# Shared expert in groups of 512 tokens with stationary first-layer weights, and the first routed expert's weights split during attention

## The chip, the cores and the metric

One NeuronCore of a Trainium2 chip runs the program. The metric is the device time of one execution in microseconds (us), and the median of three runs stands for the kernel. Before the change it is 575.73 us (575.15 to 580.42).

## The reference

A batch of 8 x 256 tokens (2048) of width D = 256 passes a gated cross-attention and then a gated mixture of experts:

```python
x = x + tanh(g_xattn) * attention(layernorm(x), ctx)      # 16 heads of 16, 77 keys per batch
n = layernorm(x).reshape(2048, 256)
w, sel = top_k(softmax(n @ gate_w.T), 2); w = w / w.sum(-1)
h = gelu(einsum('th,ehf->tef', n, W1) + b1); y = einsum('tef,efh->teh', h, W2) + b2
out = einsum('teh,te->th', y, combine(w, sel))            # 8 experts, F = 1024
out = out + gelu(n @ sW1 + sb1) @ sW2 + sb2               # shared expert, every token
x = x + tanh(g_ffn) * out
```

All is float32. The kernel computes only the two chosen experts of each token.

## The kernel before

**Attention.** It runs over 16 tiles of 128 tokens (NT = 16), software pipelined: `step(t)` on each engine does the scores of tile t + 1, the softmax of tile t, the projection of tile t - 1 and the second norm and the routing logits of tiles t - 2 to t - 4. GpSimd writes the normalised row block `x2row` (`normal_two`, L461); it first waits until the store of the block before it has landed. SP stores it to `x2`, and in the last seven steps SP also writes zeros into the DRAM tensor `routed_x`. GpSimd also loads the shared expert's weights in quarters and makes their low parts. Every weight and activation of the experts is held as a high part, rounded to fp32r, and a low part (the rest), and a product is hi x lo + hi x hi + lo x hi.

**The experts.** The work is one list of 55 tiles of 128 rows: NA = 9 early tiles of the shared expert, NR = 39 routed tiles (tokens sorted by expert in `routed_x`, padded to tiles), NB = 7 late tiles of the shared expert. All have the same form. `turn_rows` transposes the rows (L722), ACT rounds them and DVE takes the rest. `up` (L741 to L743) has the rows stationary and streams the weights: for each half of F, 2 x 3 matmuls of 512 columns. DVE adds the bias (L1277), ACT applies gelu (L1117). As the result has tokens on the partitions, `turn_hidden` transposes it in 8 pieces (L729); ACT rounds (L1111), DVE takes the rest (L1271). `down` (L754, L755) has 8 times 512 + 256 columns. `result` adds the two halves and b2 (L1387, L1394), and for shared tiles adds into `xres` (L1400). TensorE's order in a tile i is turn_hidden(i - 1), up(i), turn_rows(i + 1), down(i - 1).

**Routing.** When the last logits are copied (L1283), DVE chooses the two experts (L1373 to L1380), TensorE counts (`places`), and DVE works out the row number of each token (`slot`, L1453) between the first two early tiles. GpSimd then issues 32 indirect DMAs (L619), which scatter `x2` into `routed_x`. SP loads the first routed tile only after all 32 have landed. Routed results go to DRAM (`store_y`, L1121). When all 39 are stored, GpSimd issues 32 indirect DMAs that gather them back (L655), and DVE multiplies them by the shares and adds them (`combine`, L1416), in between the late tiles.

**First routed expert.** Its weights are loaded in quarters in the steps 9 to 14 and after the loop, and split on GpSimd after the last attention step (four quarters of `w1`, L491, and four of `w2`, L497). Later experts are loaded and split by `phase` (L506, L514) while the tiles before theirs run.

## Time and profile before

| | |
|---|---|
| device time, median of 3 runs | 575.73 us (575.15 to 580.42) |
| span of the profiled execution | 641.5 us |
| mean granted TensorE clock | 0.910 of full speed |
| TensorE matmuls busy | 551.5 us, 86% |
| VectorE busy | 357.8 us, 56% |
| ScalarE busy | 242.0 us, 38% |
| GpSimd busy | 292.1 us, 46% |
| DMA | 95.21 MB, mean 148 GB/s |

The profiled execution took its own time: its span alone is 65.8 us longer than the median of the runs, so a time of the profile is not taken over before it is known in which part of the span that difference lies. Attention takes up the first 190 us, the early shared tiles follow with the scatter, then the routed tiles, and the late shared tiles with the gather are the last 80 us.

### The profile page before, as it was taken

To read this page: it belongs to the slowest core of one execution; us is meant where nothing else is said; L and a number is where in the kernel's file an instruction comes from. 1 tells how busy PE (TensorE), PEld (TensorE's weight loads), DVE (VectorE), ACT (ScalarE), POOL (GpSimd) and SP (SyncE) were. 2 spreads that over 40 slices of the span, in tenths; PEclk is the share of its full clock that TensorE was granted. 3 is DMA by queue.
4 is the path that set the end of the run, shared out by engine and by line. 5 is a ranking of instruction groups with operands and counts; after the bars stand their busy time and mean duration, and the time that the engine had idled before them with its cause. 6 is when DMAs were issued, how large, how long until landed. Compare 5 with 4: busy or idle time off the path is not lost.

```text
span 641.5 us, 12348 instructions
## 1 busy us (share of the span) xinstructions
PE 551.5 (86%) x3243; PEld 478.4 (75%) x3244; DVE 357.8 (56%) x735; ACT 242.0 (38%) x534; POOL 292.1 (46%) x267
## 2 busy tenths in 40 slices
PE   4799899998976841999999999999999999951496
PEld 3699899998965620888888888888888888840385
DVE  4346776655639510757556565565655655520398
ACT  3123576665641200333433334333333343310132
POOL 6226478885437774004354444444545430077300
PEclk9957799989886955899999999999999999995699
DMA  4752556567846332006556678486666640143211
GB/s 131 198 167 79 157 145 172 171 188 229 255 159 203 106 107 74 16 26 216 148 200 179 206 207 237 122 245 214 185 203 180 204 114 33 41 114 105 84 50 65
DMA packets 62216, 95.21 MB, mean 148 GB/s; under 512 B 6653, under 2 KB 47853, under 8 KB 62197
## 3 DMA queue, kind: packets, MB, share of 16 engines
q0 software_dynamic: 24800, 57.82, 30.7%
q1 hardware_dynamic: 28885, 29.77, 14.5%
q10 hardware_dynamic: 8512, 7.40, 3.8%
q8 instruction: 9, 0.15, 0.1%
q14 instruction: 10, 0.08, 0.0%
HBM read 68.15 MB, written 20.71 MB: 139 GB/s over the span
## 4 chain that ended last, share of the span: by engine, by line
PE 69%; DVE 9%; issue 8%; another core or an unknown queue 7%; ACT 3%; DMA 3%; ACTq 1%; POOL 0%; DVEq 0%; SPq 0%; POOLq 0%
PE ps L754 15%; PE ps L755 7%; PE ps L741 7%; PE ps L742 7%; PE ps L743 7%; PE ps L729 7%; PE ps L812 3%; PE ps L768 3%; PE ps L707 3%; PE ps L798 2%; PE ps L780 2%; PE ps L722 2%; DVE rt L1375 1%; DMA front<-in_ctx 1%
## 5 line engine op out<-in xcount | busy, mean ns | idle before, releaser
L754 PE MATMUL ps<-w2hl,hTh 128*128 (+1 forms) x440 | 164.6, 411 | 14.0 <-DVE hTl L1271 12.7
L1117 ACT ACTIVATE hid<-hid 128x512 f32<-128x512 f32 x110 | 69.2, 632 | 161.3 <-DVE hid L1277 150.3
L755 PE MATMUL ps<-w2hl,hTl 128*128 (+1 forms) x440 | 124.9, 284 | 0.0
L1111 ACT ACTIVATE hTh<-ps 128x512 fp32r<-128x512 f32 x110 | 60.1, 597 | 132.4 <-PE ps L729 87.6
L754 PEld LDWEIGHTS ps<-w2hl,hTh 128*128 128x128 f32 x440 | 84.2, 191 | 34.2 <-issue 16.9
L1277 DVE TENSOR_TENSOR hid<-ps,b1bc 128x512 f32<-128x512 f32 x110 | 75.3, 690 | 53.9 <-PE ps L743 22.4
L741 PE MATMUL ps<-w1l,xT 128*128 (+1 forms) x220 | 94.4, 429 | 11.1 <-issue 6.6
L742 PE MATMUL ps<-w1h,xT 128*128 (+1 forms) x220 | 89.1, 405 | 3.9 <-issue 3.9
L743 PE MATMUL ps<-w1h,xT 128*128 (+1 forms) x220 | 89.0, 404 | 3.0 <-issue 3.0
L755 PEld LDWEIGHTS ps<-w2hl,hTl 128*128 128x128 f32 x440 | 84.5, 192 | 0.0
L729 PE MATMUL ps<-ident,hid 128*128 128x128 f32 x440 | 60.2, 281 | 24.8 <-ACT hid L1117 18.9
L1271 DVE TENSOR_TENSOR hTl<-ps,hTh 128x512 fp32r<-128x512 f32 x110 | 71.0, 685 | 6.0 <-issue 6.0
L729 PEld LDWEIGHTS ps<-ident,hid 128*128 128x128 f32 x440 | 51.9, 145 | 29.0 <-ACT hid L1117 20.2
L1387 DVE TENSOR_TENSOR ysum<-ps,b2bc 128x256 f32<-128x256 f32 x55 | 23.3, 424 | 78.6 <-PE ps L755 45.0
L514 POOL TENSOR_TENSOR w2hl<-stage,w2hl 128x2048 f32 (+1 forms) x8 | 36.9, 4613 | 54.9 <-DMA w2hl<-in_L_ffn_W 49.8
L741 PEld LDWEIGHTS ps<-w1l,xT 128*128 128x128 f32 x220 | 42.9, 195 | 20.9 <-issue 8.7
L506 POOL TENSOR_TENSOR w1l<-stage,w1h 128x2048 f32 (+1 forms) x8 | 36.9, 4616 | 41.9 <-DMA w1h<-in_L_ffn_W 35.8
L743 PEld LDWEIGHTS ps<-w1h,xT 128*128 128x128 f32 x220 | 42.6, 194 | 13.5 <-issue 3.0
L742 PEld LDWEIGHTS ps<-w1h,xT 128*128 128x128 f32 x220 | 43.1, 196 | 11.1 <-issue 3.4
L1265 DVE TENSOR_TENSOR xT<-ps,xT 128x256 fp32r<-128x256 f32 x55 | 23.3, 424 | 50.0 <-ACT xT L1021 44.8
L655 POOL DMA_INDIRECT gath<-routed_y,slot x32 | 30.5, 952 | 44.2 <-DMA routed_y<-yrow 34.8
L812 PEld LDWEIGHTS ps<-spread_v,probT 128*128 128x128 f32 (+1 forms) x320 | 41.4, 199 | 1.2
(178 smaller groups left out, 846.2 us busy)
## 6 DMA issues: line engine op xcount, KB each, us to landing
stage<-in_L_ffn_W POOLq DMA_DIRECT2D x14, 1024.0 KB, 6.1
w1h<-in_L_ffn_W POOLq DMA_DIRECT2D x7, 1024.0 KB, 5.9
w2hl<-in_L_ffn_W POOLq DMA_DIRECT2D x7, 1024.0 KB, 8.4
qstack<-moved_q SPq DMA_DIRECT2D x48, 128.0 KB, 2.4
xrow<-routed_x SPq DMA_DIRECT2D x39, 128.0 KB
routed_y<-yrow ACTq DMA_DIRECT2D x39, 128.0 KB, 2.3
routed_x<-zeros SPq DMA_DIRECT2D x6, 768.0 KB, 5.8
moved_q<-hid SPq DMA_DIRECT2D x16, 256.0 KB, 3.6
```

Source lines behind the costliest of these rows:

```text
L506: pool.tensor_tensor(lo, stage1[:], hi.bitcast(F32), ALU.subtract).then_inc(S["split_w1"], 1)
L729: last = nc.tensor.transpose(p_hT[:, n, c, :], hid[:, n, c * P:(c + 1) * P], ident[:])
L741: mm(p_h[:, n, :], xTh[:, c, :], part(w1l, c), start=c == 0, stop=False)
L742: mm(p_h[:, n, :], xTh[:, c, :], part(w1h, c), start=False, stop=False)
L743: last = mm(p_h[:, n, :], xTl[:, c, :], part(w1h, c), start=False, stop=c == C - 1)
L754: mm(p_y, hTh[:, c, :], part(2 * D), start=c == 0, stop=False)
L755: last = mm(p_y[:, 0:D], hTl[:, c, :], part(D), start=False, stop=c == FC - 1)
L812: last = mm(p_o[:, h0:h1, :], probT[0:n, j, :], spread_v[0:n, at:at + h1 - h0, bass.ds(t // TB, 1), :].rearrange("k n o d -> k (n o) d"), ...
L1111: act.activation(hTh[:, n * (FC // 2):(n + 1) * (FC // 2), :], p_hT[:, n, :, :], ACT.Copy).then_inc(S["hT_hi"], 1)
L1117: act.activation(hid[:, n, :], hid[:, n, :], ACT.Gelu).then_inc(S["h_act"], 1)
L1271: tt(hTl[:, part, :], p_hT[:, n, :, :], hTh[:, part, :].bitcast(F32), ALU.subtract).then_inc(S["hT_lo"], 1)
L1277: tt(hid[:, n, :], p_h[:, n, :], b1bc[:, bass.ds(s, 1), n * (F // 2):(n + 1) * (F // 2)].rearrange("p o f -> p (o f)"), ALU.add).then_inc( ...
```

## The change

- The shared expert works in 4 groups of 512 tokens (`WIDE_T` = 4 tiles), two groups in front of the routed tiles and two behind: the 9 + 7 tiles become 8 + 8. Within a group it goes over the 8 chunks of F; a step g is one chunk of one group, 16 steps early and 16 late.
- `wide_up(g)` has a 128 x 128 chunk of the first layer's weights stationary and streams 512 tokens, 6 matmuls. The result has F on the partitions, so it is not transposed. ACT adds the bias in the gelu, from PSUM to PSUM in place, and rounds it to `hTh` (`wide_gelu`, `wide_round`); DVE takes the rest (`wide_rest`). `wide_down(g)` adds the chunk's part to four PSUM banks, 4 x (512 + 256) columns. `wide_result` and `wide_add` finish a group's four tiles.
- `turn_wide(w)` transposes 4 tiles straight from `x2`, without SP's loads of `xrow`. Group 0 is turned in the last attention step, group 1 in its tail, groups 2 and 3 in early steps 8 and 14.
- The routing code on DVE is cut up between the first early `wide_rest`s.
- The first routed expert's remaining quarters are loaded in the steps 13 and 14 and split in the steps 13 to 16 (L491 in 13 and 14, L497 in 15 and 16). The load of the second expert's first layer into `stage1` moves to step 15. Its `fill` begins once the early steps' matmuls are done instead of at the first routed tile.
- The routed tiles run as before.

The core of the diff (renamed counters, buffers and semaphores are left out):

```diff
-    NA = NT // 2 + 1
-    NB = NT - NA
+    WIDE_T = 4
+    NW = NT // WIDE_T
+    EARLY = NW // 2
+    WQ = WIDE_T * P
+    NG = NW * FC
+    G1 = EARLY * FC
...
+        py_banks = (7, 2, 3, 4)
+        wide_banks = ((1, 2), (3, 4), (5, 6), (5, 6))
...
             sp.wait_ge(S["scattered"], 16 * TOP * NT)
-            in_pairs(sp, R0, R1, lambda i, parity: load_rows(i, parity, "routed"))
-            sp.wait_ge(S["x2_out"], 16 * NT)
-            in_pairs(sp, R1, TILES, lambda i, parity: load_rows(i, parity, "late"))
+            load_rows(0, 0)
+            load_rows(1, 1)
+            in_pairs(sp, 2, NR, load_rows)
...
-                    load_b1(0, shared_b[0])
-                    load_b2(0, shared_b[1])
+                    pool.dma_start(sb1T[:], sb1.rearrange("(c p) -> p c", p=P), allow_slow_non_contiguous=True
+                                   ).then_inc(S["sb1_in"], 16)
+                    load_b2(0, shared_b2)
...
-                    load_quarter_2(1, first_w2, t - 13)
+                    load_quarter_2(1, first_w2, 2 * (t - 13))
+                    load_quarter_2(1, first_w2, 2 * (t - 13) + 1)
+                    split_quarter_1(1, 2 * (t - 13))
+                    split_quarter_1(1, 2 * (t - 13) + 1)
+                if t == 15:
+                    pool.wait_ge(S["split_w1"], 8)
+                    load_w1(2, expert_w1(1))
+                    ready_1(1)
+                if 15 <= t < 17:
+                    split_quarter_2(1, 2 * (t - 15))
+                    split_quarter_2(1, 2 * (t - 15) + 1)
 
             for t in range(NT + 2):
...
-            load_quarter_2(1, first_w2, 2)
-            load_quarter_2(1, first_w2, 3)
-            for q in range(4):
-                split_quarter_1(1, q)
-            pool.wait_ge(S["split_w1"], 8)
-            load_w1(2, expert_w1(1))
-            ready_1(1)
-            for q in range(4):
-                split_quarter_2(1, q)
             pool.wait_ge(S["split_w2"], 8)
             load_w2(2, expert_w2(1))
             ready_2(1)
...
+                if halves is None:
+                    pool.wait_ge(S["sh_ps"], G1)
+                else:
+                    met(pool)
+                    pool.wait_ge(S["h_add"], halves)
                 load_hi1(s, here[0])
...
+            fill(2, 0, expert_b(1), (expert_w1(1), expert_w2(1)), (expert_w1(2), expert_w2(2)))
             pool.wait_ge(S["tables_set"], 1)
-            with pool.Fori(2, E) as p:
+            with pool.Fori(3, E) as p:
...
+            def turn_wide(w):
+                pe.wait_ge(S["x2_out"], 16 * WIDE_T * (w + 1))
+                if w == 0:
+                    pe.wait_ge(S["p_sub"], NT)
+                elif w == 1:
+                    pe.wait_ge(S["pt_sb"], 3 * NT)
+                else:
+                    pe.wait_ge(S["wx_lo"], 2 * w)
+                    pe.wait_ge(S["slots_set"], 1)
+                for c in range(C):
+                    for j in range(WIDE_T):
+                        last = nc.tensor.transpose(ps[:, wide_banks[w][c], j * P:(j + 1) * P],
+                                                   x2[:, w * WIDE_T + j, c * P:(c + 1) * P], ident[:])
+                    last.then_inc(S["wx_ps"], 1)
+
+            def wide_up(g):
+                w, m, s = g // FC, g % FC, 0 if g < G1 else (PH - 1) % 2
+                pe.wait_ge(S["w1_ready"], 1 if g < G1 else PH)
+                pe.wait_ge(S["wx_lo"], 2 * w + 2)
+                if g >= 2:
+                    pe.wait_ge(S["sh_lo"], g - 1)
+                if G1 <= g < G1 + 2:
+                    pe.wait_ge(S["h_add"], 2 * NR - 1 + g - G1)
+                bank = ps[:, g % 2, :]
+                for c in range(C):
+                    part = lambda wt: wt[:, s, c, m * P:(m + 1) * P]
+                    hi, lo = xTs[:, w % 2, 0, c, :], xTs[:, w % 2, 1, c, :]
+                    mm(bank, part(w1l), hi, start=c == 0, stop=False)
+                    mm(bank, part(w1h), hi, start=False, stop=False)
+                    last = mm(bank, part(w1h), lo, start=False, stop=c == C - 1)
+                last.then_inc(S["sh_ps"], 1)
+
+            def wide_down(g):
+                w, m, s = g // FC, g % FC, 0 if g < G1 else (PH - 1) % 2
+                pe.wait_ge(S["sh_lo"], g + 1)
+                pe.wait_ge(S["w2_ready"], 1 if g < G1 else PH)
+                for j, b in enumerate(py_banks):
+                    if g == 0 and j == 0:
+                        pe.wait_ge(S["o_norm"], NT)
+                        pe.wait_ge(S["wx_lo"], 4)
+                    if m == 0 and w >= 1:
+                        pe.wait_ge(S["sh_sum"], WIDE_T * (w - 1) + j + 1)
+                    if g == G1 and b == 4:
+                        pe.wait_ge(S["y_sum"], NR)
+                    at = slice(j * P, (j + 1) * P)
+                    mm(ps[:, b, :], half_of(hTh, g)[:, at], w2hl[:, s, m, :], start=m == 0, stop=False)
+                    last = mm(ps[:, b, 0:D], half_of(hTl, g)[:, at], w2hl[:, s, m, 0:D],
+                              start=False, stop=m == FC - 1)
+                    if m == FC - 1:
+                        last.then_inc(S["sh_y"], 1)
+                if m < FC - 1:
+                    last.then_inc(S["sh_down"], 1)
...
+                    turn_wide(0)
                 if ok(t):
                     turn_probs(t, 0)
...
-                    up(0, 0, 0)
+                    wide_up(0)
...
+            wide_up(1)
+            step(NT + 1, 1)
+            turn_wide(1)
+            step(NT + 2, 0)
+            step(NT + 3, 1)
...
+            for g in range(G1):
+                wide_down(g)
+                if g + 2 < G1:
+                    wide_up(g + 2)
+                if g == 1:
+                    places()
+                if g == 8:
+                    turn_wide(2)
+                if g == G1 - 2:
+                    turn_wide(3)
...
+            up(0, *phase_at(0))
             turn_rows(1, 1)
-            tile(1, 1, (0, 0), (0, 0), places)
-            in_pairs(pe, 2, R0, lambda i, parity: tile(i, parity, (0, 0), (0, 0)))
-            pe.wait_ge(S["tables_set"], 2)
-            tile(R0, R0 % 2)
-            in_pairs(pe, R0 + 1, TILES - 1, tile)
-            tile(TILES - 1, (TILES - 1) % 2)
-            tile(TILES, TILES % 2)
+            tile(1, 1)
+            in_pairs(pe, 2, NR - 1, tile)
+            tile(NR - 1, (NR - 1) % 2)
+            turn_hidden(NR - 1)
+            wide_up(G1)
+            down(NR - 1, *phase_at(NR - 1))
+            wide_up(G1 + 1)
+            for g in range(G1, NG):
+                wide_down(g)
+                if g + 2 < NG:
+                    wide_up(g + 2)
...
+            def wide_gelu(g):
+                act.wait_ge(S["sh_ps"], g + 1)
+                act.activation(ps[:, g % 2, :], ps[:, g % 2, :], ACT.Gelu, bias=sb1T[:, g % FC:g % FC + 1]
+                               ).then_inc(S["sh_act"], 1)
+
+            def wide_round(g):
+                act.wait_ge(S["sh_act"], g + 1)
+                if g >= 2 and (g - 2) % FC == FC - 1:
+                    act.wait_ge(S["sh_y"], WIDE_T * ((g - 2) // FC + 1))
+                elif g >= 2:
+                    act.wait_ge(S["sh_down"], (g - 2) // FC * (FC - 1) + (g - 2) % FC + 1)
+                if g == G1:
+                    act.wait_ge(S["y_ps"], NR)
+                act.activation(half_of(hTh, g), ps[:, g % 2, :], ACT.Copy).then_inc(S["sh_hi"], 1)
...
+            act.wait_ge(S["sb1_in"], 16)
+            wide_gelu(0)
+            step(NT + 2)
+            wide_round(0)
...
+            for g in range(1, G1):
+                wide_gelu(g)
+                wide_round(g)
+                if g == 4:
+                    share_tanh()
+                if g == 10:
+                    wide_hi(2)
+            wide_hi(3)
+            rows_hi(0)
+            gelu(0)
+            rows_hi(1)
+            tile(1, store=False)
+            each(act, 2, NR - 1, tile)
+            tile(NR - 1)
+            hidden_hi(NR - 1)
+            store_y(NR - 2)
+            wide_gelu(G1)
+            wide_round(G1)
+            store_y(NR - 1)
...
+            def wide_rest(g):
+                dve.wait_ge(S["sh_hi"], g + 1)
+                tt(half_of(hTl, g), ps[:, g % 2, :], half_of(hTh, g).bitcast(F32), ALU.subtract
+                   ).then_inc(S["sh_lo"], 1)
...
+            wide_hi(1)
+            step(NT + 2)
+            wide_lo(1)
+            step(NT + 3)
+            wide_rest(0)
...
+            def wide_result(w, j):
+                n, s = w * WIDE_T + j, 0 if w < EARLY else (PH - 1) % 2
+                dve.wait_ge(S["sh_y"], n + 1)
+                if w >= 1:
+                    dve.wait_ge(S["y_added"], n - WIDE_T + 1)
+                tt(ywide[:, j, :], ps[:, py_banks[j], 0:D], b2bc[:, s, :], ALU.add).then_inc(S["sh_mid"], 1)
+                dve.wait_ge(S["sh_mid"], n + 1)
+                tt(ywide[:, j, :], ps[:, py_banks[j], D:2 * D], ywide[:, j, :], ALU.add).then_inc(S["sh_sum"], 1)
+
+            def wide_add(w, j):
+                t = w * WIDE_T + j
+                dve.wait_ge(S["sh_sum"], t + 1)
+                if w == NW - 1:
+                    dve.wait_ge(S["g_done"], j + 1)
+                stt(xres[:, t, :], ywide[:, j, :], tgate[:, 1:2], xres[:, t, :], ALU.mult, ALU.add
+                    ).then_inc(S["out_ready" if w == NW - 1 else "y_added"], 1)
...
+            dve.memset(chosen[:], 0.0)
+            dve.wait_ge(S["l_sb"], NT)
+            dve.wait_ge(S["far_set"], 1)
+            choose(0)
+            wide_rest(1)
+            choose(1)
+            mark_chosen()
+            wide_rest(2)
+            slots()
+            wide_rest(3)
+            tables()
+            wide_rest(4)
+            tile_phases()
+            wide_rest(5)
+            shares()
+            wide_rest(6)
+            wide_rest(7)
+            for g in range(FC, G1):
+                if g == FC:
+                    wide_result(0, 0)
+                wide_rest(g)
+                if g == FC:
+                    for j in range(1, WIDE_T):
+                        wide_result(0, j)
+                    for j in range(WIDE_T):
+                        wide_add(0, j)
+                if g == 10:
+                    wide_lo(2)
+            wide_lo(3)
+            for j in range(WIDE_T):
+                wide_result(1, j)
+            for j in range(WIDE_T):
+                wide_add(1, j)
+            rows_lo(0)
...
+            COMBINED = {4: (0, 1), 6: (2, 3), 8: (4, 5), 10: (6, 7), 12: (8, 9), 14: (10, 11), 15: (12, 13)}
+            for g in range(G1, NG):
+                if g == G1 + FC:
+                    wide_result(EARLY, 0)
+                wide_rest(g)
+                if g == G1 + FC:
+                    for j in range(1, WIDE_T):
+                        wide_result(EARLY, j)
+                    for j in range(WIDE_T):
+                        wide_add(EARLY, j)
+                for t in COMBINED.get(g - G1, ()):
+                    combine(t)
+            combine(14)
+            combine(15)
+            for j in range(WIDE_T):
+                wide_result(NW - 1, j)
+                wide_add(NW - 1, j)
```

## Rows read from the trace of the kernel before

**Rows 1.** The page, section 2: TensorE's granted clock in 40 slices of the span.

```profile
PEclk9957799989886955899999999999999999995699
```

**Rows 2.** Table by stretches: microseconds, each engine's busy time (and instructions), clock, DMA.

```profile
219.70:257.40 37.70, 11.63 (x38) 7.78 (x38) 6.54 (x13) 3.79 (x7) 23.35 (x25) 0.63 0.26 94
...
563.10:606.50 43.40, 15.75 (x62) 10.81 (x60) 7.13 (x14) 3.68 (x7) 27.91 (x30) 0.67 0.34 96
```

**Rows 3.** Timeline of VectorE: start, length, instruction; four tiles' results.

```profile
218.02 0.43 DVE L1394 TENSOR_TENSOR yrow<-ps,ysum 128x256 f32<-128x256 f32 x1
...
255.74 0.42 DVE L1394 TENSOR_TENSOR yrow<-ps,ysum 128x256 f32<-128x256 f32 x1
...
563.77 0.42 DVE L1394 TENSOR_TENSOR yrow<-ps,ysum 128x256 f32<-128x256 f32 x1
...
606.05 0.42 DVE L1394 TENSOR_TENSOR yrow<-ps,ysum 128x256 f32<-128x256 f32 x1
```

**Rows 4.** Timeline of VectorE and GpSimd: row numbers, first and last of 32 scatters and gathers.

```profile
209.04 0.18 DVE L1453 CAST slot<-posf 128x32 int32<-128x32 f32 x1
...
209.52 1.09 POOL L619 DMA_INDIRECT routed_x<-x,slot  x1 [4.67 <-DVE slot L1453]
...
249.39 0.97 POOL L619 DMA_INDIRECT routed_x<-x,slot  x1 [0.30 <-issue]
...
559.94 1.02 POOL L655 DMA_INDIRECT gath<-routed_y,slot  x1 [34.80 <-DMA routed_y<-yrow]
...
598.90 0.95 POOL L655 DMA_INDIRECT gath<-routed_y,slot  x1 [0.30 <-issue]
```

**Rows 5.** Timeline of GpSimd and VectorE during the choice of experts.

```profile
191.76 5.05 POOL L491 TENSOR_TENSOR w1l<-stage,w1h 128x512 fp32r<-128x512 f32 x4
...
191.80 2.63 DVE L1375 TENSOR_TENSOR rt<-logits,top 128x128 f32<-128x128 f32 x1
...
197.97 5.02 DVE L1375 TENSOR_TENSOR rt<-lg,top 128x128 f32<-128x128 f32 x1
203.03 0.29 DVE L1376 TENSOR_TENSOR rt<-rt,iota_far 128x128 f32<-128x128 f32 x1
```

**Rows 6.** Groups by line: out<-in, shapes, count, busy us, mean ns, idle before and releaser.

```profile
L1117 ACT ACTIVATE hid<-hid 128x512 f32<-128x512 f32 x110 | 69.2, 632 | 161.3 <-DVE hid L1277 150.3
L1111 ACT ACTIVATE hTh<-ps 128x512 fp32r<-128x512 f32 x110 | 60.1, 597 | 132.4 <-PE ps L729 87.6
...
L1271 DVE TENSOR_TENSOR hTl<-ps,hTh 128x512 fp32r<-128x512 f32 x110 | 71.0, 685 | 6.0 <-issue 6.0
...
L1416 DVE SCALAR_TENSOR_TENSOR xres<-gath,share,xres 128x256 f32<-128x256 f32 x32 | 14.9, 481 | 0.6
```

**Rows 7.** Timeline of TensorE and ACT's queue over one routed tile.

```profile
549.71 1.03 PE L729 MATMUL ps<-ident,hid 128*128 128x128 f32 x8
550.50 0.48 PE L741 MATMUL ps<-w1l,xT 128*128 x1
...
553.52 0.48 PE L754 MATMUL ps<-w2hl,hTh 128*128 x1
...
556.41 1.03 PE L729 MATMUL ps<-ident,hid 128*128 128x128 f32 x8
...
557.96 0.34 ACTq L1121 DMA_DIRECT2D routed_y<-yrow  x1
```

**Rows 8.** Timelines of GpSimd, VectorE and TensorE: attention and the first early tile.

```profile
79.01 1.22 POOL L461 TENSOR_SCALAR x2row<-xres,mv,nw 128x256 f32<-128x256 f32 x1 [5.99 <-ACT nw L1044]
...
169.26 1.22 POOL L461 TENSOR_SCALAR x2row<-xres,mv,nw 128x256 f32<-128x256 f32 x1 [5.85 <-DMA x<-x2row]
...
191.28 0.17 DVE L1283 COPY logits<-ps 128x8 f32<-128x8 f32 x1 [2.52 <-PE ps L841]
...
197.85 0.77 PE L741 MATMUL ps<-w1l,xT 128*128 128x512 f32 x1 [3.79 <-POOLq L528]
```

**Rows 9.** DMA issues: count, size, median us from issue to landing.

```profile
x<-x2row SPq DMA_DIRECT2D x16, 128.0 KB, 2.1
```

282 lines of the change are left out of this document (134 added, 148 removed).

## The prediction

> **What bounds the kernel now.** I first asked where the profiled execution lost its 65.8 us against the median. The table by stretches shows two stretches, 219.7 to 257.4 us and 563.1 to 606.5 us, in which TensorE is busy 11.63 of 37.7 and 15.75 of 43.4 us at a granted clock of 0.63 and 0.67 while GpSimd is busy for most of them [rows 2]; the clock row dips in those slices [rows 1]. The timeline says what they are: both begin some 3 to 10 us after the first of 32 indirect DMAs and end some 5 us after the last [rows 4]. Two shared tiles' results lie 255.74 - 218.02 = 37.7 us apart in the first and 606.05 - 563.77 = 42.3 us in the second [rows 3], where a routed tile takes 556.41 - 549.71 = 6.70 us [rows 7]. The loss is 31.0 + 35.6 = 66.6 us, and 641.5 - 66.6 = 574.9 us, 0.8 us under the median. So I take it that the stall belongs to the profiled execution, and count without it: times after the first stretch less 31.0 us, after the second less 66.6 us, and 0.8 us on the final span. That the DMAs' own pace is the same in the unprofiled runs is an assumption.
>
> Counted so, the indirect DMAs matter in another way. The row numbers are there at 209.2; the 32 scatters go from 209.5 to 250.4, one each 1.28 us [rows 4]; with 2.1 us for the last to land and 2.1 us for SP's first load [rows 9] the first routed rows are there at 254.6. TensorE would turn them at 254.5: the last store of a routed tile is issued at 557.96 - 31.0 = 527.0, the first 38 x 6.70 = 254.6 us before that, at 272.4. In the steady pattern rows are turned just ahead of the `down` at 553.5, and the store of that tile comes two periods after 557.96, 17.9 us later [rows 7]. So the scatter ends as TensorE needs it. The gathers start at 559.94 - 31.0 = 528.9, take 39.9 us [rows 4], and with landing 2.1, two combines of 2 x 0.48 = 1.9, a tile's result 1.4 (2 x 0.42 + 0.5) [rows 3, 6] and the store's landing 2.1 [rows 9] end at 576.3, 1.4 us over the 574.9 that TensorE's seven late tiles also reach. Both ends of the shared work are balanced: TensorE and the chain of the 32 DMAs finish together. In between, TensorE is full.
>
> **What the change takes off TensorE.** The columns of the first and second layer per 128 tokens stay the same. From the timeline `up` with the next rows takes 3.0 us, and of the tile's 6.70 us the 8 hidden transposes take 0.8 to 1.0 us (549.71 to 550.50) [rows 7]. `down` then has 6.70 - 3.0 - 0.8 = 2.9 us. A wide step has 6 of the 12 matmuls of `up`, 1.4 us, and 24 / 48 of `down`'s parts, 1.4 us: 2.8 us for a quarter-width of F over 4 tiles, thus 8 x 2.8 / 4 = 5.6 us per tile against 6.7. Over 16 tiles TensorE loses 17 us of work. Whether that reaches the end depends on the DMA chain, which the change doesn't shorten by itself.
>
> **Does the wide loop hold 2.8 us a step?** Two PSUM banks alternate. From the end of up(g) to down(g) there is one down and one up, 2.8 us; in it lie gelu, round and rest: 0.6 + 0.6 + 0.69 [rows 6] plus three handovers that I put at 0.1, 2.2 us. It holds with 0.6 us to spare. A gelu from PSUM to PSUM is not in the trace; the nearest are 0.60 (PSUM to SBUF) and 0.63 (SBUF to SBUF), and I take 0.6, with 0.4 to 1.9 for the bounds (three times the row). The loop slips where DVE is held by other work: choice, row numbers and tables (some 3 us in all beyond the spare), and at a change of group, where down(8) waits bank by bank for results of 0.9 us each and step 9's rest for four adds of 0.5 us: 3 us, once early and once late.
>
> **The row numbers.** Before, the choice of experts ran beside the splits on GpSimd: one comparison took 2.63 and another 5.02 us beside splits of 5.05 and of the same kind again, and 0.29 us is what such an operation takes when GpSimd is quiet [rows 5]. All 17.8 us from the last logits (191.4, [rows 8]) to `slot` (209.2) shrink. The new chain by steps: rest(0) 0.7 to 192.1; down(0) and up(2), at the lower clock after the pause, 2.6 each, to 197.3 (the same matmul takes 0.77 us at 197.85 and 0.48 in the steady tile [rows 7, 8]); down(1) and up(3) 2.8 to 200.1; the count 0.7; ten small DVE operations 2.5: 203.3. DVE itself would have chosen by 197 and isn't the late one; TensorE's order is. In front of that, attention's last step: 6 transposes more (+0.6), six matmuls fewer ahead of the heads' transposes of tile 15 (-1.4): -0.8. Against it stands the moved work on GpSimd: in steps 13 and 14 four issues of loads (I put them at 0.8 each) and two splits of 1.3 (a quarter of 5.05 [rows 5]) are 5.8 us behind a `normal_two` of 1.2 [rows 8]. Who is queued behind: `normal_two` of the next tile, and for it turn_x2, the logits and DVE's moments. `normal_two` already waits 5.85 us for its predecessor's store [rows 8], which shares the DMA rings with 768 KB of zeros and now with 512 KB more of weights. I bound this by 0 and 3 us in all four steps together reaching the end (a late store in one step uses up waits of the next), and take 0.5. `slot` is written at 203, 6.2 us earlier (201 to 206).
>
> Where the splits now stand, DVE's operations could be held as the comparison was; the nearest bounds are 0 and 2.6 us a step. I take 0, since the steps 5 to 12 of before hold such splits already, and what was held in the trace is the comparison, with both inputs in SBUF. The Trainium skill, page "SBUF — State Buffer", section "Who interferes with whom", says that a DVE instruction with two SBUF inputs contends with a GpSimd instruction that reads SBUF, and one with a single SBUF input outside the two-port modes doesn't; the comparisons have two, and the trace agrees with it (5.02 against 0.29 us). By that rule the moved splits cost attention nothing as well, since its DVE operations read PSUM or one SBUF tensor.
>
> The tiny strided load of sb1 replaces a 512 KB broadcast in step 0; GpSimd waits 5.99 us in the third step after it [rows 8], which hides up to that much; I take 0, and 2 us without that cover.
>
> **The sum.** From `slot` at 203: scatters 41.2 with the handover, landing 2.1, first load 2.1: rows there at 248.4. TensorE's 16 early steps (from 192.1: 2 downs at low clock, 14 x 2.8, two turns of 0.9, 6 us of slips) end at about 241, and DVE's results and adds behind them at 246: hidden by the scatter, 2 us to spare. TensorE stands 7 us, so the first routed tile starts at the lower clock. Its way alone through the pipeline (turn, hi, lo 1.5; up 2.8 + 2.0 for the clock; bias and gelu 1.4; turn 0.8; up 3.0; down 2.9; result and handover 1.3) is 15.7 us: first store at 264.1. 38 x 6.70 = 254.6, less 1.6 as the last tile has half an `up` beside it: last store 517.1. Before it was 527.0.
>
> Then store and handover 2.0, 32 gathers 39.9, landing 2.1, two combines 1.9, four results with adds 4 x 1.4 = 5.6 (they stand behind the last combine on DVE), store 2.1: 570.7. TensorE's own late part, from the last `down` at 515.8: 1.6 + 16 downs and 14 ups of 1.4 + 3 of slips = 46.6, to 562.4, with results 5.6 and store 2.1: 570.1. Again both ends meet. Counted in the same way, before was 576.3 where 574.9 is the span; I take that 1.4 off, add 0.8 for the median: 570.1. One more landing and load is in the chain at the scatter, which the same estimate sizes 1.1 us too high. The forecast is **569.0 us**, 1.2% less than 575.73. A measurement of this kernel tells no less than about 1% from no change.
>
> **The rivals.**
> (a) TensorE is the bound. If the indirect DMAs run faster unprofiled, the scatter no longer holds the first tile: up(0) at 246, no low clock, first store at 258.6, last at 511.6, end at 564. For it: in the profiled execution something costly hangs on just these DMAs. Against: their pitch is the same with stalled and running engines. The full 17 us with no slips would give 558.4.
> (b) The moved loads and splits hold back attention's tail. The 5.85 us wait becomes 7 to 9 us in steps 13 to 16, and `slot` comes at 206 to 209: 572 to 576 us. For it: `normal_two` is late already. Against: no quarter is loaded after step 14, and ACT's chain sets the last two steps if GpSimd is through by then.
> (c) The change doesn't pay: scatter and gather alone set the time and `slot` isn't earlier, as places stands behind four wide steps at the lower clock and four results stand behind the last combine: 576 us.
> (d) Slower. The place is the two-bank loop of the wide steps. If gelu in PSUM, round and rest with handovers take more than 2.8 us, every step pays the excess e, 14 times late in full and 14 times early less the 7 us that the scatter hides: 28e - 7. At e = 0.7 (a gelu of 1.9 us) that is 13 us, 582 us; at e = 1.0, 590 us. It decides from a step of 3.5 us on. For it: the form isn't in the trace. Against: both neighbours take 0.6 us.
>
> **How the numbers follow.** My forecast's case has 0.50 (565 to 573; three fifths of it under 570.0, the 1% bound). (a) 0.22, all faster. (b) 0.13 and (c) 0.07, within 1%. (d) 0.08, slower. Faster: 0.30 + 0.22 = 0.52; within 1%: 0.20 + 0.13 + 0.07 = 0.40; slower 0.08. The range leaves out (d) and the full 17 us: 560 to 576.5.
>
> **What would show it.** In the new profile: `slot` near 203 and comparisons of 0.29 us; wide steps of 2.8 us; the first routed load right after the last scatter has landed; 6.70 us per routed tile; the first gather 2 us after the last store, and combine(15) after the last gather, four results behind it. The profiled execution will again hold stalls beside the indirect DMAs, over more of the wide steps, and its span will be over 600 us; only the milestones before and between tell. The prediction is wrong if the routed tiles start later than `slot` + 61 us with their first store, if a wide step takes over 3 us, or if the stall turns out to be in the unprofiled runs too.

## The result and the profile after

The changed kernel takes 582.87 us (median of 20 runs, 579.27 to 590.41), the kernel before, over as many runs, 580.79 us (575.15 to 587.90). The ratio is 1.0076, with a 95% interval of 1.0046 to 1.0106; all ratios here compare only runs within 1.5% of their kernel's fastest, and the medians of all runs would give 1.0036. The interval leaves out 1, so the changed kernel is a little slower, by less than the 1% that I had named as the bound; 569.0 us was forecast, and the time lies outside the range of 560 to 576.5. A part of the miss is the time that I started from: 575.73 us was the median of three runs, and twenty give 5 us more. The ratio is free of that.

The profiled execution of the changed kernel took 582.31 us, with a span of 580.6 us. The page, section 2, its clock row:

```profile
PEclk9775989999899699959999999999999999999998
```

There is no hole in it like the two of [rows 1]; the 5 in its 18th slice is the second stretch of the next table. This table goes by stretches of the same trace, over the scatter and over the start of the routed tiles (columns as in [rows 2]):

```profile
200.00:240.00 40.00, 39.33 (x212) 32.28 (x212) 19.89 (x49) 17.75 (x31) 26.04 (x27) 1.00 0.24 85
247.00:262.00 15.00, 6.64 (x20) 4.92 (x20) 2.17 (x5) 1.01 (x2) 7.96 (x6) 0.54 0.61 204
```

TensorE is busy for 39.33 of 40 us beside the scatters, at a granted clock of 1.00. The stall of [rows 2] is absent. Instead TensorE is busy 6.64 of 15 us just behind the scatters, at a clock of 0.54.

The choice of experts and the row numbers, timeline of VectorE in the kernel after (answers to [rows 4, 5, 8]):

```profile
193.20 0.17 DVE L1437 COPY logits<-ps 128x8 f32<-128x8 f32 x1 [2.97 <-PE ps L924]
...
194.23 0.29 DVE L1529 TENSOR_TENSOR rt<-logits,top 128x128 f32<-128x128 f32 x1
...
196.77 0.29 DVE L1529 TENSOR_TENSOR rt<-lg,top 128x128 f32<-128x128 f32 x1
...
198.06 0.29 DVE L1537 TENSOR_TENSOR chosen<-hot 128x128 bf16<-128x128 f32 x1
...
205.56 0.18 DVE L1603 CAST slot<-posf 128x32 int32<-128x32 f32 x1
```

The comparisons of 2.63 and 5.02 us are down to 0.29. From the last logits to `slot` it is 12.36 us against 17.76. But the choice stands at 198.06 and its count doesn't come before 202.4:

```profile
199.31 0.63 PE L833 MATMUL ps<-w2hl,hTh 128*128 128x512 f32 x1
...
202.39 0.23 PE L1014 MATMUL ps<-chosen,before 128*128 128x136 bf16 x1
```

This is the timeline of TensorE; between the two rows it does `wide_down(1)` and `wide_up(3)`.

The hand-over to the routed tiles, timelines of GpSimd, SP and TensorE in the kernel after:

```profile
245.85 0.96 POOL L632 DMA_INDIRECT routed_x<-x,slot  x1 [0.31 <-issue]
246.81 0.78 POOL L475 DMA_DIRECT2D w1h<-in_L_ffn_W  x1
247.56 0.64 POOL L530 DMA_DIRECT2D b1bc<-in_L_ffn_b  x1
...
248.32 1.14 SPq L330 DMA_DIRECT2D xrow<-routed_x  x2
...
254.23 0.66 PE L748 MATMUL ps<-ident,xrow 128*128 128x128 f32 x2 [11.24 <-DMA xrow<-routed_x]
```

Right behind its last scatter GpSimd issues the 1 MB of the next expert's weights and the 512 KB bias, 1.5 us ahead of SP's first load of rows, which now takes 5.9 us to the transpose that waits for it. TensorE stands for 11.24 us, and its matmuls before had ended at 243.0.

The end, timelines of VectorE and GpSimd in the kernel after:

```profile
523.80 0.42 DVE L1546 TENSOR_TENSOR yrow<-ps,ysum 128x256 f32<-128x256 f32 x1
...
526.23 1.02 POOL L679 DMA_INDIRECT gath_a<-routed_y,slot  x1 [32.46 <-DMA routed_y<-yrow]
...
566.10 0.95 POOL L679 DMA_INDIRECT gath_b<-routed_y,slot  x1 [0.30 <-issue]
...
568.85 0.69 DVE L1414 TENSOR_TENSOR hTl<-ps,hTh 128x512 fp32r<-128x512 f32 x1 [0.27 <-ACT hTh L1139]
569.46 3.74 DVE L1578 SCALAR_TENSOR_TENSOR xres<-gath_b,share,xres 128x256 f32<-128x256 f32 x8
573.12 0.42 DVE L1557 TENSOR_TENSOR ywide<-ps,b2bc 128x256 f32<-128x256 f32 x1
...
577.97 0.48 DVE L1566 SCALAR_TENSOR_TENSOR xres<-ywide,tgate,xres 128x256 f32<-128x256 f32 x1
```

Behind the last wide step's `wide_rest` VectorE has 9 us of work in a row: four `combine`s (3.74 us) and twelve operations of four tiles' results (573.12 to 578.45).

### The profile page after: what moved, and what is told of

The parts are those of the page before. It is cut to its first block, busy times and chain, and to the rows that moved or that the text cites. A ratio compares the mean times of both kernels' runs of the same rounds, so it can differ in the third digit from the quotient of the medians.

```text
span 580.6 us, 11601 instructions
## 1 busy us (share of the span) xinstructions
PE 529.0 (91%) x3115; PEld 459.2 (79%) x3116; DVE 327.6 (56%) x697; ACT 242.9 (42%) x524; POOL 292.6 (50%) x266
## 4 chain that ended last, share of the span: by engine, by line
PE 69%; DMA 7%; POOL 7%; DVE 5%; issue 5%; ACT 4%; ACTq 1%; SPq 1%; DVEq 0%; POOLq 0%
PE ps L784 13%; PE ps L771 7%; PE ps L785 6%; PE ps L773 6%; PE ps L772 6%; PE ps L757 6%; POOL routed_x L632 5%; PE ps L731 3%; PE ps L851 3%; PE ps L833 3%; PE ps L895 2%; PE ps L881 2%; DMA x<-x2row 2%; DMA moved_q<-hid 2%; PE ps L748 2%
## 5 line engine op out<-in xcount | busy, mean ns | idle before, releaser
L784 PE MATMUL ps<-w2hl,hTh 128*128 x312 | 114.8, 407 | 0.0
L785 PE MATMUL ps<-w2hl,hTl 128*128 x312 | 87.7, 281 | 0.0
L1431 DVE TENSOR_TENSOR hid<-ps,b1bc 128x512 f32<-128x512 f32 x78 | 53.8, 691 | 30.2 <-PE ps L773 25.0
L784 PEld LDWEIGHTS ps<-w2hl,hTh 128*128 128x128 f32 x312 | 58.7, 188 | 12.6 <-issue 0.3
L771 PE MATMUL ps<-w1l,xT 128*128 x156 | 66.0, 423 | 1.5 <-DVE xT L1419 1.5
L524 POOL TENSOR_TENSOR w2hl<-stage,w2hl 128x2048 f32 (+1 forms) x8 | 36.9, 4613 | 51.6 <-DMA w2hl<-in_L_ffn_W 46.9
L773 PE MATMUL ps<-w1h,xT 128*128 x156 | 62.5, 400 | 0.0
L772 PE MATMUL ps<-w1h,xT 128*128 x156 | 62.4, 400 | 0.0
L785 PEld LDWEIGHTS ps<-w2hl,hTl 128*128 128x128 f32 x312 | 59.1, 189 | 0.0
L833 PE MATMUL ps<-w2hl,hTh 128*128 128x512 f32 x128 | 49.0, 413 | 5.0 <-DVE hTl L1414 4.3
L1414 DVE TENSOR_TENSOR hTl<-ps,hTh 128x512 fp32r<-128x512 f32 x32 | 22.0, 689 | 36.2 <-ACT hTh L1139 36.0
L632 POOL DMA_INDIRECT routed_x<-x,slot x32 | 31.3, 979 | 21.4 <-DVE slot L1603 12.0
L895 PE MATMUL ps<-spread_v,probT 128*128 (+4 forms) x320 | 38.6, 269 | 0.0
```

Source lines behind the costliest of these rows:

```text
L632: pool.indirect_dma_start(out=rows, out_offset=bass.IndirectOffsetOnAxis(ap=slot[:, k, t:t + 1], axis=0), in_=x2[:, t, :], in_offset=None) ...
L771: mm(p_h[:, n, :], xTh[:, c, :], part(w1l, c), start=c == 0, stop=False)
L772: mm(p_h[:, n, :], xTh[:, c, :], part(w1h, c), start=False, stop=False)
L773: last = mm(p_h[:, n, :], xTl[:, c, :], part(w1h, c), start=False, stop=c == C - 1)
L784: mm(p_y, hTh[:, c, :], part(2 * D), start=c == 0, stop=False)
L785: last = mm(p_y[:, 0:D], hTl[:, c, :], part(D), start=False, stop=c == FC - 1)
```

## How the runs are compared

In the profiles TensorE's clock falls to the lower of its two levels in different places of attention from one execution to the next. For runs without a profile only the mean clock is on record: over the runs of the kernel before it went from 0.935 to 0.967, and the whole time from 591 to 571 us, some 5 us for each 0.01. I therefore read each profile from the last logits on, in four stages between starts in its timelines: last copy of `logits`, `slot`, first routed `yrow`, first gather, last operation on `xres`. The ratios are to runs of the kernel before on the same chip, and hold attention as well. Each line is one profiled execution. How far these agree is seen where the same code recurs: the front is 64.77 to 65.39 us in the four kernels with the wide form and all DMAs but without the late fill, and 60.98 to 61.55 us in the four with it; the end is 51.68 to 53.32 us in five and 47.32 to 47.49 in the four with the short tail. All in us; a name is that of the run below.

```
                     to slot  to 1st yrow  to gather  to last xres  sum     ratio (95%)
before, repeated      17.54     63.32       257.35     44.84       383.05   0.9968 (0.9915-1.0021)
after                 12.36     65.30       255.37     51.74       384.77   1.0076 (1.0046-1.0106)
late fill             11.21     60.98       255.41     53.32       380.92   1.0052 (1.0014-1.0089)
splits put back       16.80     65.39       255.41     53.24       390.84   1.0153 (1.0082-1.0225)
results first         11.36     64.92       255.37     52.78       384.43   1.0126 (1.0074-1.0178)
before, half          17.56     61.78       258.29     42.99       380.62   0.9947 (0.9904-0.9989)
after, half           11.27     60.71       255.37     51.68       379.03   0.9977 (0.9930-1.0025)
before, splits moved   9.79     62.58       258.54     44.91       375.82   0.9918 (0.9870-0.9966)
late fill, short tail 11.70     61.44       255.37     47.32       375.83   0.9915 (0.9878-0.9952)
short tail            11.58     64.77       255.43     47.43       379.21   0.9966 (0.9920-1.0012)
+ early ranks          9.75     61.55       255.42     47.49       374.21   0.9896 (0.9824-0.9968)
+ rows first           9.58     61.38       255.42     47.38       373.76   0.9877 (0.9821-0.9934)
```

## The experiments

**The kernel before, repeated.** No edit.

> The kernel before, profiled anew. The ratio to itself should be 1.000 within half a per cent, which sizes the noise. Theory A (the stall beside the indirect DMAs belongs to the one profiled execution, and not to the kernel): a span of 575 to 586 us with no stretch beside the scatter or the gather in which TensorE waits for 30 us; the row numbers at 209 to 214 us, the first gather some 320 us after them. Theory B (the kernel has the stall and the changed one has not): a span over 620 us again, and then the device time of this execution over 620 us too. The distance from the last logits to the row numbers should be 17.8 us again (comparisons beside the splits of 2.6 and 5 us), from the row numbers to the last result's store some 367 us.

It has no stall: its profiled execution took 575.07 us, with a span of 573.5. Over the scatter, table by stretches of the repeated kernel before:

```profile
208.00:248.00 40.00, 40.00 (x228) 34.36 (x227) 28.70 (x62) 15.74 (x30) 29.46 (x31) 1.00 0.33 115
```

40.00 of 40 us, where [rows 2] has 11.63 of 37.7. The 66.6 us belonged to that one execution. Here is the path of the repeated one, timelines of VectorE:

```profile
187.80 0.17 DVE L1283 COPY logits<-ps 128x8 f32<-128x8 f32 x1 [2.34 <-PE ps L841]
...
188.32 2.42 DVE L1375 TENSOR_TENSOR rt<-logits,top 128x128 f32<-128x128 f32 x1
...
194.28 5.02 DVE L1375 TENSOR_TENSOR rt<-lg,top 128x128 f32<-128x128 f32 x1
...
205.34 0.18 DVE L1453 CAST slot<-posf 128x32 int32<-128x32 f32 x1
...
268.66 0.42 DVE L1394 TENSOR_TENSOR yrow<-ps,ysum 128x256 f32<-128x256 f32 x1
...
570.85 0.48 DVE L1400 SCALAR_TENSOR_TENSOR xres<-yrow,tgate,xres 128x256 f32<-128x256 f32 x1
```

And its hand-over to the routed tiles, timelines of SP, TensorE and GpSimd:

```profile
248.36 9.75 SPq L316 DMA_DIRECT2D xrow<-routed_x  x4
...
250.46 0.44 PE L722 MATMUL ps<-ident,xrow 128*128 128x128 f32 x2 [1.07 <-DMA xrow<-routed_x]
...
251.01 0.75 POOL L465 DMA_DIRECT2D w1h<-in_L_ffn_W  x1 [4.41 <-DVE hid L1277]
```

Against it the kernel after gains 5.18 us to `slot`, loses 1.98 to the first `yrow`, gains 1.98 over the routed tiles, and loses 6.90 behind the first gather: 1.7 us in sum.

**Late fill.** GpSimd waits with the second expert's loads until the first routed rows are turned.

```diff
                 if halves is None:
                     pool.wait_ge(S["sh_ps"], G1)
+                    pool.wait_ge(S["xT_ps"], 1)
```

> The changed kernel, in which the fill for the second routed expert (1.5 MB of loads) waits until TensorE has turned the first routed rows. Theory A (the fill's loads, issued 1.5 us ahead of the first load of routed rows, share the DMA rings with it, and it lands after 5.8 us where such a load alone takes 2.2): the load lands 3.6 us earlier, the first routed tile and everything up to the last store move by 3.6 us, ratio to before some 1.001 where the changed kernel has 1.0076. Theory B (the 5.8 us are those of a first read of rows just scattered, not of the fill): no change in the load, ratio 1.007 to 1.009. If expert 2's weights come too late for its first tile, a gap of some us appears in the routed part, which would raise the ratio.

Its first load of rows is issued 2.47 us after the last scatter's start, at 251.27, as in the kernel after, and its rows are turned 2.04 us later, timeline of TensorE with the late fill:

```profile
253.31 0.66 PE L749 MATMUL ps<-ident,xrow 128*128 128x128 f32 x2 [7.38 <-DMA xrow<-routed_x]
```

The first `yrow` comes 60.98 us after `slot` instead of 65.30. So 4.3 us of the front were the weights' DMAs ahead of the rows. The end took 1.6 us of it back (53.32 instead of 51.74): the last gather started at 564.72, 1.4 us sooner than in the kernel after, but TensorE's late wide steps ran from 553 to 557 us at a clock of 0.57, and ended at the same time as there. Two more profiles have such a stretch just there: 0.57 with the splits put back and 0.64 with the results first. In all three the last `wide_rest` starts 44.1 to 44.2 us after the first gather, in the kernel after 42.6. The stretch is no effect of the late fill, then. The ratio of 1.0052 lies between my two theories, and its interval holds the 1.0076 of the kernel after: the stage shows the gain, the whole time doesn't.

**Splits put back.** The loads and splits of the first expert as before, the wide form kept.

```diff
-                    load_quarter_2(1, first_w2, 2 * (t - 13))
-                    load_quarter_2(1, first_w2, 2 * (t - 13) + 1)
-                    split_quarter_1(1, 2 * (t - 13))
-                    split_quarter_1(1, 2 * (t - 13) + 1)
-                if t == 15: ...
-                if 15 <= t < 17: ...
+                    load_quarter_2(1, first_w2, t - 13)
             for t in range(NT + 2):
                 step(t)
+            load_quarter_2(1, first_w2, 2)
+            ...
+            for q in range(4):
+                split_quarter_1(1, q)
```

> The changed kernel with the loads and splits of the first routed expert back behind the last attention step, as in the kernel before. Theory A (the moved splits and loads hold back attention's last steps by what is queued behind them, and the choice of experts gains by them): the last logits come 2 to 3 us earlier relative to the attention step 12, but the choice is held beside the splits by 8 us, in part hidden behind TensorE's first two steps, so the row numbers come 2 to 5 us later and the ratio is 1.010 to 1.016. Theory B (moving the splits is a loss, as TensorE's order sets the row numbers and not the choice): ratio 1.002 to 1.006.

It takes 16.80 us from logits to `slot`, 4.4 us more than the kernel after, and the slow comparisons are back, timeline of VectorE with the splits put back:

```profile
199.69 2.57 DVE L1528 TENSOR_TENSOR rt<-logits,top 128x128 f32<-128x128 f32 x1
...
206.10 4.76 DVE L1528 TENSOR_TENSOR rt<-lg,top 128x128 f32<-128x128 f32 x1
```

The ratio of 1.0153 is what the wide form costs alone, from six runs; the interval of 1.0082 to 1.0225 leaves out 1. The last logits don't come sooner, as the first theory had it: they come 36.2 us behind the twelfth `x2row`, with TensorE at a mean clock of 0.72 in attention's tail (last section).

**Results first.** The last group's four results ahead of `combine(14)` and `combine(15)`, their adds behind.

```diff
+            for j in range(WIDE_T):
+                wide_result(NW - 1, j)
             combine(14)
             combine(15)
             for j in range(WIDE_T):
-                wide_result(NW - 1, j)
                 wide_add(NW - 1, j)
```

> The changed kernel with the last group's four results taken ahead of the last two combines, so that four adds alone stand behind the last gather's combines. Theory A (VectorE's queue behind the last gather sets the end): of 5.3 us behind the last combine 3.4 go ahead of the last gather's landing where the last down steps are done by then; TensorE's last step ends only 1 to 2 us after the last gather has landed, so 1.5 to 3 us are won, ratio 1.003 to 1.005. Theory B (TensorE's last step sets the end): less than 1 us, ratio 1.006 to 1.008.

Behind the first gather it takes 52.78 us against 51.74, and the ratio of 1.0126 is above what either theory gave. But the stretch at the lower clock lies in this end as well and costs 1.5 us of it. From the last `wide_rest` to the last `xres` it is 8.61 us (574.43 to 583.04), against 9.12 in the kernel after: the order gains 0.5 us, where I had hoped for 1.5 to 3. VectorE's work stays nearly the same in sum; it must become less, or go elsewhere.

**Half the indirect DMAs, in both kernels.** They leave out the scatter and the gather of the second choice's rows, and `combine` reads the first choice's rows for both, so the output is not that of the reference.

```diff
-            sp.wait_ge(S["scattered"], 16 * TOP * NT)
+            sp.wait_ge(S["scattered"], 16 * NT)
...
-                for k in range(TOP):
+                for k in range(1):
```

> The kernel before with one scatter and one gather for each tile of tokens instead of two (16 and 16 indirect DMAs in all; the rows of the second choice are neither scattered nor gathered, and the sum reads the first choice's rows for both). It takes some 20 us off the scatter and 20 us off the gather. Theory 1 (the kernel before is bound by TensorE at both ends, with 1.07 us of waiting for the first routed rows in its repeated profile and the last routed sums done before the last result): the time falls by 1 to 3 us, ratio to before 0.995 to 0.999. Theory 2 (the chain of indirect DMAs is the bound, so that TensorE only fills time): 10 to 25 us less, ratio 0.96 to 0.98.

> The same halving of scatters and gathers in the kernel after. Theory 1 (the 17 us taken off TensorE in the shared tiles are idle time in front of the first routed rows and behind the last wide step, so that a shorter scatter brings the front part back): TensorE no longer waits 5 to 11 us for the first routed rows and no longer falls to the low clock there; the first store of routed results comes 7 to 11 us sooner after the slot numbers, the end by the same amount, ratio to before 0.988 to 0.996. Theory 2 (the wide form of the shared expert doesn't save TensorE time): as the kernel after, ratio 1.005 to 1.01.

The kernel before gets 2.4 us shorter (1.5 to the first `yrow`, 1.9 at the end, 0.9 given back between), though 40 us of indirect DMAs are gone. So the chain of DMAs outlasts its TensorE work by no more than 1.5 and 1.9 us at the two ends; that part of my reading holds. The kernel after gets 5.7 us shorter, and 65.30 - 60.71 = 4.6 of them in front, less than the 7 to 11 expected. Its end is as long as with all gathers, timelines of GpSimd and VectorE:

```profile
519.84 1.02 POOL L679 DMA_INDIRECT gath_a<-routed_y,slot  x1 [33.82 <-DMA routed_y<-yrow]
...
538.98 0.94 POOL L679 DMA_INDIRECT gath_b<-routed_y,slot  x1 [0.30 <-issue]
...
571.52 0.48 DVE L1566 SCALAR_TENSOR_TENSOR xres<-ywide,tgate,xres 128x256 f32<-128x256 f32 x1
```

The last gather starts 19.1 us after the first instead of 39.9, and the end takes 51.68 us against 51.74. So it is not the gathers that set the end of the kernel after, but TensorE's late wide steps (42.56 us to the last `wide_rest`, 42.62 with all gathers) and VectorE's 9.1 us behind it.

In front, with the rows there early, something else holds them, timelines of VectorE and TensorE in the kernel after with half the DMAs:

```profile
244.23 4.74 DVE L1566 SCALAR_TENSOR_TENSOR xres<-ywide,tgate,xres 128x256 f32<-128x256 f32 x4
248.89 0.41 DVE L1419 TENSOR_TENSOR xT<-ps,xT 128x256 fp32r<-128x256 f32 x1
...
249.55 0.79 PE L771 MATMUL ps<-w1l,xT 128*128 x1 [7.84 <-DVE xT L1419]
```

Four adds of the wide tile take 4.74 us (1.66 in the kernel after) beside GpSimd's split, which runs from 243.00 for 4.49 us, and the rows' low part stands behind them on VectorE. TensorE waits 7.84 us, again at the change from wide to routed. The Trainium skill, page "SBUF — State Buffer", section "Who interferes with whom", says that a VectorE instruction with two SBUF inputs contends with a GpSimd instruction that reads SBUF. These adds read `ywide` and `xres`, both in SBUF, and the trace agrees: 4.74 against 1.66 us.

**The moved splits alone, in the kernel before.**

```diff
-                    load_quarter_2(1, first_w2, t - 13)
+                    load_quarter_2(1, first_w2, 2 * (t - 13))
+                    load_quarter_2(1, first_w2, 2 * (t - 13) + 1)
+                    split_quarter_1(1, 2 * (t - 13))
+                    split_quarter_1(1, 2 * (t - 13) + 1)
+                if t == 15: ...
+                if 15 <= t < 17: ...
...
-            load_quarter_2(1, first_w2, 2)
-            load_quarter_2(1, first_w2, 3)
-            for q in range(4):
-                split_quarter_1(1, q)
...
```

> The kernel before with one part of the change alone: the first expert's second-layer loads two quarters a step in steps 13 and 14, its first-layer splits in steps 13 and 14, its second-layer splits in steps 15 and 16. Theory 1 (the slot numbers come 5 to 6 us sooner after the last logits, but TensorE's early tiles end when they did): the end moves by -2 to +2 us, ratio 0.997 to 1.003. Theory 2 (my forecast's price, the chain from the slot numbers sets the end): 5 us less, ratio 0.990 to 0.993.

0.9918: the change's small part is a gain of 0.8%. That is the second of the two theories, the price of my forecast. Timeline of VectorE in this kernel:

```profile
192.80 0.17 DVE L1284 COPY logits<-ps 128x8 f32<-128x8 f32 x1 [5.27 <-PE ps L842]
...
195.60 0.29 DVE L1376 TENSOR_TENSOR rt<-lg,top 128x128 f32<-128x128 f32 x1
...
197.19 1.28 DVE L1272 TENSOR_TENSOR hTl<-ps,hTh 128x512 fp32r<-128x512 f32 x2
...
202.59 0.18 DVE L1454 CAST slot<-posf 128x32 int32<-128x32 f32 x1
```

`slot` comes 9.79 us after the logits, 7.75 sooner than in the repeated kernel before. TensorE isn't left behind as I thought: its first early tile had also stood behind the slow comparisons. The `hTl` of that tile comes 4.4 us after the logits instead of 12.8 (187.80 to 200.60). Both chains of the front, TensorE's and that of the DMAs, start behind the choice, so both gain.

The move has a price in attention. From one `x2row` of GpSimd to the next there lie, in the kernel after:

```profile
172.28 1.22 POOL L471 TENSOR_SCALAR x2row<-xres,mv,nw 128x256 f32<-128x256 f32 x1 [1.97 <-DMA x<-x2row]
173.46 0.76 POOL L495 DMA_DIRECT2D stage<-in_L_ffn_W  x1
...
176.41 2.51 POOL L501 TENSOR_TENSOR w1l<-stage,w1h 128x512 fp32r<-128x512 f32 x2
178.92 1.21 POOL L471 TENSOR_SCALAR x2row<-xres,mv,nw 128x256 f32<-128x256 f32 x1
```

6.64 us without a pause: GpSimd is the bound of this step. In the repeated kernel before it was 4.2 us, in the one with half the DMAs 3.7. Some 2.5 us, then, and the ratios agree: from the logits on the kernel before with moved splits gains 7.2 us on the repeated one, in the whole 0.8% or 4.7 us. That is an inference from one step and from two sorts of measurement. From the twelfth `x2row` to the last logits it takes 28.5 to 30.6 us in the three profiles without the moved splits and 29.6 to 31.4 in the six with them that don't have attention's low clock (last section), so single profiles don't separate the price from the spread.

**Late fill and short tail; short tail alone.** One pair of sums less behind the last wide step, and the last four tiles' second bias added in step 10, so that a result is two operations (`last_half`, one for each half of the bank). `add_b2` adds tanh(g) times the bias to `xres` ahead of them.

```diff
+            def last_half(j, k):
...
+                stt(xres[:, t, :], ps[:, py_banks[j], k * D:(k + 1) * D], tgate[:, 1:2], xres[:, t, :],
+                    ALU.mult, ALU.add).then_inc(S["out_ready" if k else "sh_mid"], 1)
...
-            COMBINED = {4: (0, 1), 6: (2, 3), 8: (4, 5), 10: (6, 7), 12: (8, 9), 14: (10, 11), 15: (12, 13)}
+            COMBINED = {3: (0, 1), 5: (2, 3), 7: (4, 5), 9: (6, 7), 11: (8, 9), 13: (10, 11), 14: (12, 13)}
...
+                if g - G1 == 10:
+                    add_b2()
             combine(14)
             combine(15)
-            for j in range(WIDE_T):
-                wide_result(NW - 1, j)
-                wide_add(NW - 1, j)
+            for k in range(2):
+                for j in range(WIDE_T):
+                    last_half(j, k)
```

> The kernel after with the late fill of the weights, and with VectorE's work behind the last wide step cut: pairs of sums moved to steps 3, 5, 7, 9, 11, 13 and 14, so that one pair is left behind it instead of two (1.9 us less), and the second bias of the last four tiles added in step 10, so that a result is two instructions and not three (1.6 us less). Theory 1 (VectorE's serial tail sets the end, with the last gather already landed): from the last logits to the last result 377 to 379 us, against 381.4 with the late fill alone and 383.6 in the kernel before; ratio to before 0.996 to 1.001. Theory 2 (the last gather or TensorE's last wide step sets the end): within 1 us of the late fill alone, ratio 1.004 to 1.006.

> The kernel after with VectorE's shortened tail alone, without the late fill. Theory 1 (the loss of the wide form has two places, 6.9 us behind the last gather and some 4 us in front of the first routed rows): from the first gather's start to the last store's issue 48 us as with both edits (52.2 in the kernel after), and from the slot numbers to the first store of routed results still 65 to 66 us; ratio to before 0.998 to 1.003. Theory 2 (with the front late, TensorE's last wide step ends later too and swallows the shorter tail): 50 us or more, ratio over 1.003.

The end with both, timeline of VectorE:

```profile
563.53 0.69 DVE L1415 TENSOR_TENSOR hTl<-ps,hTh 128x512 fp32r<-128x512 f32 x1 [0.24 <-ACT hTh L1140]
565.12 1.92 DVE L1598 SCALAR_TENSOR_TENSOR xres<-gath_b,share,xres 128x256 f32<-128x256 f32 x4 [0.90 <-DMA gath_b<-routed_y,slot]
566.96 3.22 DVE L1585 SCALAR_TENSOR_TENSOR xres<-ps,tgate,xres 128x256 f32<-128x256 f32 x8
```

Now VectorE waits 0.90 us for the last gather, and 5.1 us of work follow instead of 9. Behind the first gather it takes 47.32 us, and 47.43 without the late fill: 4.4 us less than the kernel after in either. And without the late fill the front keeps its 64.77 us. The two losses are separate, and their edits add up: -3.9 in front and -4.4 behind. Of the 4.4 us, 2.95 lie behind the last `wide_rest` (6.17 us instead of 9.12). The other 1.5 were not in the plan, which had 3.5 in all: with the pairs of sums one step earlier TensorE waits 0.2 us for the low part at the late change of group, where it waited 2.1. None of the four kernels with this tail has the stretch at the lower clock there. The two kernels' ratios, 0.9966 and 0.9915, are 1.1% and 1.6% under that of the kernel after, and under the 0.998 to 1.003 and 0.996 to 1.001 that I expected.

**Early ranks, and rows first.** The count of ranks behind `wide_down(0)` and `wide_up(2)`; then also the first routed rows' low parts ahead of the second wide tile's adds.

```diff
-                if g == 1:
+                if g == 0:
                     places()
```
```diff
+            rows_lo(0)
             for j in range(WIDE_T):
                 wide_add(1, j)
-            rows_lo(0)
```

> Late fill and short tail, and the count of ranks on TensorE one wide step sooner (behind the first step's products instead of the second's). Theory 1 (from the last logits to the slot numbers the wide kernels need 11.7 to 12.4 us against 9.8 in the kernel before with the moved splits, because TensorE reaches the count 3 us after the choice is marked): 9 to 10 us from last logits to slot numbers and 2 us less in the end, ratio 0.986 to 0.990. Theory 2 (VectorE's hand-over at the end of the early tiles holds the first routed rows instead): slot numbers sooner, the first store no sooner, ratio 0.990 to 0.993.

> As the kernel with the early ranks, and on VectorE the first routed rows' low parts ahead of the four sums of the second wide tile instead of behind them (in the kernel after with half the scatters these four took 4.74 us beside GpSimd's split instead of 1.66, and TensorE waited 7.84 us for the rows). Theory 1 (with sooner slot numbers the sums would hold the rows): up to 2 us less than with the early ranks alone, ratio 0.984 to 0.989. Theory 2 (the rows still come after the sums are done): the same as with the early ranks alone within 0.5 us.

The ranks' step takes the logits to `slot` from 11.70 to 9.75 us, and most of it arrives: 374.21 in sum against 375.83. The rows' order changes nothing (61.38 against 61.55 us), since the rows come after the adds (with the early ranks the adds end at 250.0 and the rows are turned at 251.86); this is Theory 2 of that run. The last kernel has the lowest ratio of all, 0.9877, but its interval overlaps those of the others with a short tail and that of the kernel before with the moved splits. The stages tell them apart, the whole times don't.

## Why the prediction was wrong

The sum went from `slot` at 203 to 570.7 us. Term by term, against the kernel after:

- The choice of experts: right. From the logits to `slot` I had 11.9 us (191.4 to 203.3), and it is 12.36. TensorE's order was the late one, as forecast; moving the count one step forward brought 2 us. What I didn't ask is whether it need be so: the moved splits alone give 9.79.
- From `slot` to the first store 61.1 us were forecast, with one load of 2.1 us. It is 65.85 us; my sum was 4.7 too short, 3.3 of it up to the rows' transpose and 1.5 behind it, where the first tile's way, put at 15.7 us, took 17.2. **This step failed**: "the first routed load right after the last scatter has landed", at 2.1 us. It does come there, but behind 1.5 MB of weights and bias that GpSimd issued just before it. In the repeated kernel before, GpSimd's load of that expert waited for the last early tile (251.01, behind a wait on VectorE's `hid`), and the rows were turned at 250.46, 2.1 us after their load at 248.36. `fill(2, ...)` waits on `sh_ps` instead, which the last early wide step has raised before the last scatter is out; I had read its wait as one that is always met early and not asked what it then lets go ahead. The late fill sizes it at 4.3 us. The early wide steps didn't enter: they ended 49.8 us after the last logits, for which the forecast has 49.6 (191.4 to 241), though its terms as written add up to 244.3.
- The routed tiles: right. First to last store 253.0 forecast, 252.85 measured, at 6.70 us each.
- The end: the first gather comes 2 us after the last store, as forecast. From the first gather's start to the end of the last one's issue I had 39.9 us, and it is 40.8 (526.23 to 567.05). Behind the last gather's landing I had two combines and four results, 7.5 us. VectorE does four combines, 3.74 us, and four results of 1.31 each: 9.0 us. The term of 1.9 us for two combines was mis-sized by 1.8, as `combine(12)` and `(13)` also stand behind the last `wide_rest`, and the results were 0.4 better. From the last store to the end of the span it is 56.3 us (524.26 to 580.6) against my 53.6, which was itself 5.7 over the 47.9 of before. Both ends met in my sum, TensorE's at 570.1 and the gathers' at 570.7. With half the gathers the end is as long, so the binding one is TensorE's, behind which I had results only and not the four combines.
- Attention: I took 0.5 us for the moved splits out of 0 to 3, and 0.8 off for fewer matmuls. By the ratios it cost about 2.5 us, near the upper bound of 3. Rival (b) was right that the moved work holds attention's tail, but not by its mechanism: the wait for the block before, 5.85 us there, didn't grow to 7 to 9 but shrank to 1.97 and to nothing, as GpSimd itself is busy. VectorE's operations beside the moved splits were not held, as forecast (`o_n` takes 0.42 us at 168.06 beside a split, as at 162.18 without one, in the trace of the kernel after). The row to go by would have been the issues and splits themselves: four issues and two splits, 5.5 us behind an `x2row` of 1.2, make 6.6 us of GpSimd alone, more than the 3.7 to 5.8 us that the step took.
- The corrections: after the sum I took 1.4 us off because the same sum came out over the span before, and 1.1 more for the scatter. Both made the forecast lower without a mechanism. Without them the sum says 4.2 us less than before, not 6.7.
- The baseline: 5 us too low with three runs.

From the logits on I had -5.9 to `slot`, -2.1 to the first store, -1.6 over the routed tiles and +5.7 behind them, -3.9 in all; measured are -5.2, +2.0, -2.0 and +6.9, in all +1.7. The stage that turns the sign is the one from `slot` to the first store, with 4.1 of the 5.6 us of difference, and the late fill, which only clears the way of the first load, gives back 4.3; the end adds 1.2.

Where did the 17 us of TensorE go? They are real: a wide step has a pitch of 2.8 us (`wide_rest` at 563.26, 566.06 and 568.85 in the kernel after), the gelu in PSUM takes 0.66 us, and rival (d) is out. But seven late tiles became eight, 7 x 6.70 = 46.9 us against 8 x 5.6 = 44.8, so only 2.1 us fell to the end. There more is lost than that: from the first gather to the last low part it takes 42.62 us against 39.99 in the repeated kernel before, and from there to the last `xres` 9.12 against 4.85. The other 15 us fell to the front, where 32 scatters last 41 us; TensorE stood 11.24 us there and began the routed tiles at the low clock. Rival (c) was the nearest in the outcome: the change doesn't pay, the scatter sets the front and four results stand behind the last combine. It erred in what `slot` gains, and in the gather, which doesn't set the end. Rival (a) needed faster indirect DMAs, and the stall that spoke for it wasn't there.

## What to carry to other kernels

Before taking work off a full engine, see whether a chain of the same length runs beside it in each stage; if so, the work can come back as idle time, and a wide form adds a drain and a fill at each change of stage, in which another engine's serial work is bare. In a change of several parts, run each alone: here one part was worth -0.8% and the other +1.5%, and the sum looked like nothing. When a queue's wait is released, look at what the other queues issue in the same microsecond, not only at how long the transfer took in quieter rows.
